# Fused adaLN, attention-like mixer and mixture-of-experts kernel: the last four tiles kept on chip for the shared expert, their reload taken out, and three orders of work moved

## The chip, the cores and the metric

The kernel runs on one core of one Trainium2 chip. The metric is device time in microseconds of one execution. Engines are named as in the profile: PE (TensorE), DVE (VectorE), ACT (ScalarE), POOL (GpSimd), SP (SyncE, which here only issues transfers).

## The reference, cut to what matters

There are 2048 tokens of 512 values, 8 experts of which each token takes 2, and a shared expert of twice an expert's hidden width (2 x 352). All is float32.

```python
mod = (_silu(L0_c) @ L0_wmod).reshape(L0_c.shape[0], 6, 1, -1)
sa, ca, ga, sb, cb, gb = ...
h = _layernorm(x, axis=-1) * (1 + ca) + sa
x = x + ga * _L0_attn_ref(h, B, C, D)     # tanh(h B^T) C^T + D * h
h = _layernorm(x, axis=-1) * (1 + cb) + sb
x = x + gb * _L0_ffn_ref(h, ...)
# in _L0_ffn_ref:
scores = jax.nn.sigmoid(logits)
_, idx = jax.lax.top_k(scores + router_bias, K)
y = jnp.einsum('eth,ehd->etd', jax.nn.silu(h1) * h3, W2)
out = jnp.einsum('etd,te->td', y, gate_full) + shared
```

## The kernel before

Tokens are cut into 16 tiles of 128, and tiles into 8 pairs. Each float32 product is made of three matmuls on a high and a low part (high x high, high x low, low x high), so every operand is held twice: `xah`, `xal` or `thi`, `tlo` (also called `xbh`, `xbl`) for tokens, `whi`, `wlo` for weights.

The program has an opening (modulation vectors, weights of the first stages) and then four stages.

**Stage A** runs over the pairs, as a software pipeline of 11 rounds (`body(it, lo, hi)` on each engine, `it` from 0 to 10). In round `it` the engines normalise pair `it`, turn the normalised pair `it - 1` and compute its states (`turn_t`, `states`), make the mixer's output for pair `it - 2` (`attention`), and for pair `it - 3` turn the second normalisation `h2` and run the first half of the shared expert (`up("A", ...)`, `down("A", ...)`, with the router's columns beside the up product). Rounds 3, 4, 8, 9 and 10 are written out, rounds 5 to 7 are a loop. `h2` of each pair goes to DRAM (`hs_rows`), comes back, and is scattered by GpSimd to rows sorted by expert (`xs_rows`, four indirect transfers a pair). The turned `h2` in its two parts goes to DRAM too (`store_x` to `xt_high`, `xt_low`).

**Stage B** runs the second half of the shared expert on four tiles, here tiles 0 to 3, which `load_x` fetches from `xt_high` and `xt_low`: two at the start of round 10, the third when the first tile's up product is done, and the fourth after the second's.

**Stage S** runs the routed experts on blocks of 128 rows of `xs_rows`, two steps in a loop. **Stage C** runs the second half of the shared expert on the other 12 tiles, fetches for each tile its two routed results (`gather`), combines and stores. The four tiles of stage B and the last two of stage C are combined apart: `gather_first` fetches their routed rows, `weigh` on ACT multiplies the first by its weight, and three operations on DVE (`combine`) end them.

A step of stages B, S and C is on PE: the up product of tile n (24 matmuls), the down product of tile n - 1 (9 matmuls), the turn of the gated hidden values of tile n (3 transposes). In stage S the turn of the next block (4 transposes) stands ahead of it. ACT makes silu and the high part of the hidden values, DVE the product and the low part. The order on each engine is written by hand, and semaphores alone order the engines.

In the profile, the up product is lines 1007 to 1009, the down product 1038 to 1040, the turn of the hidden values 1045, all other transposes 984, the mixer's products 953 to 955, and the modulation 962. The wait that guards a fetched tile is the first line of `up`:

```python
if loaded is not None:
    pe.wait_ge(q["C", "xin"][j], loaded * 32)
```

On ACT the turned pair may be overwritten in `xah` once `store_x` has read it:

```python
if lo > 3:
    act.wait_ge(q["A", "up"], p * 2)
    act.wait_ge(s_xts, p * 32)
```

## Time and profile before

| What | Value |
|---|---|
| median of 3 runs | 570.36 us (569.66 to 571.24) |
| profiled execution: its time | 571.33 us |
| its span, first to last instruction | 569.7 us |
| PE busy | 543.4 us (95%) |
| DVE, POOL, ACT busy | 286.6, 263.5, 176.3 us |
| mean granted TensorE clock | 0.990 of full |
| transfers | 119.80 MB, mean 210 GB/s |

PE is busy for 95% of the span, so the time is that of PE's work and of the gaps in it. A gap is seen as a small digit of PE in the 40 slices of the page, as less than the length of a stretch in its busy time, and in the list of PE's instructions as the number in brackets behind the instruction that came late, with what released it. "issue" in a bracket means that the profile names no releaser. A matmul's duration in such a list is longer than the distance to the next start, since matmuls overlap, so paces are read from starts.

### The profile page before, as it was taken

The numbers are of one execution on the slowest core, as the hardware profiler recorded it, in microseconds if no ns is written. First come the engines' busy times: TensorE is split into PE (matmuls) and PEld (weight loads), VectorE is DVE, ScalarE is ACT, GpSimd is POOL, SyncE is SP. The second block draws the span as 40 slices with busy tenths as digits, with TensorE's granted clock in tenths as the row PEclk, the third lists the DMA queues.
The fourth block names the chain that finished last, engine by engine and source line by source line (L and its number), as shares of the span: only waits on it lengthen the run. The fifth ranks groups of instructions, "written<-read, shape, count | busy, mean of one in ns | idle before, by whom it ended". The sixth has DMA issues, their size and how long they took to land.

```text
span 569.7 us, 11068 instructions
## 1 busy us (share of the span) xinstructions
PE 543.4 (95%) x3129; PEld 487.3 (86%) x3130; DVE 286.6 (50%) x612; ACT 176.3 (31%) x337; POOL 263.5 (46%) x221
## 2 busy tenths in 40 slices
PE   8996899999999995999999999999999999988997
PEld 3665788998999894999999999999999999987896
DVE  3788586686687565442222222222222222158897
ACT  1444345445534330122223222322223223112211
POOL 2599877668666457343016260044443300254630
PEclk9999899999999998999999999999999999999999
DMA  8999266543452889566254946255758313475982
GB/s 309 395 337 382 84 212 249 186 160 116 166 191 106 286 316 375 190 220 227 96 161 157 326 138 231 74 175 192 288 167 310 129 55 110 152 257 188 314 306 79
DMA packets 47915, 119.80 MB, mean 210 GB/s; under 512 B 4752, under 2 KB 5008, under 8 KB 47888
## 3 DMA queue, kind: packets, MB, share of 16 engines
q1 hardware_dynamic: 35088, 67.02, 33.4%
q0 software_dynamic: 12800, 52.43, 26.0%
q8 instruction: 15, 0.25, 0.2%
q14 instruction: 12, 0.10, 0.1%
HBM read 80.38 MB, written 39.06 MB: 210 GB/s over the span
## 4 chain that ended last, share of the span: by engine, by line
PE 79%; POOL 7%; issue 5%; DMA 4%; DVE 3%; ACT 1%; SPq 0%; POOLq 0%; DVEq 0%; ACTq 0%
PE bank L1007 14%; PE bank L1009 14%; PE bank L1008 14%; PE bank L1038 8%; PE bank L1040 7%; PE bank L1039 7%; PE bank L984 4%; PE bank L1045 4%; PE bank L955 2%; PE bank L953 2%; PE bank L954 2%; DMA x_all<-wmod 2%; POOL tmpa L595 1%; DMA xt_low<-xal 1%; POOL x_all L598 1%
## 5 line engine op out<-in xcount | busy, mean ns | idle before, releaser
L1007 PE MATMUL bank<-whi,thi 128*128 (+1 forms) x416 | 139.9, 336 | 8.3 <-issue 8.3
L1008 PE MATMUL bank<-wlo,thi 128*128 (+1 forms) x416 | 135.9, 327 | 0.0
L1009 PE MATMUL bank<-whi,tlo 128*128 (+1 forms) x416 | 135.5, 326 | 0.0
L582 POOL TENSOR_TENSOR wlo<-raw,whi 128x1408 f32 (+3 forms) x24 | 79.6, 3329 | 83.7 <-DMA whi<-w_all 74.0
L1007 PEld LDWEIGHTS bank<-whi,thi 128*128 128x128 f32 x416 | 79.5, 191 | 9.0 <-issue 9.0
L1742 DVE TENSOR_TENSOR gbuf<-s,bank 128x352 f32<-128x352 f32 x52 | 27.0, 520 | 112.5 <-ACT s L927 111.5
L1038 PE MATMUL bank<-whi,gth 128*128 (+1 forms) x201 | 79.9, 397 | 2.3 <-DVE gtl L1305 1.3
L1040 PE MATMUL bank<-whi,gtl 128*128 (+1 forms) x201 | 79.0, 393 | 0.0
L1008 PEld LDWEIGHTS bank<-wlo,thi 128*128 128x128 f32 x416 | 79.0, 190 | 0.0
L1009 PEld LDWEIGHTS bank<-whi,tlo 128*128 128x128 f32 x416 | 78.9, 190 | 0.0
L1039 PE MATMUL bank<-wlo,gth 128*128 (+1 forms) x201 | 78.8, 392 | 0.0
L927 ACT ACTIVATE s<-bank 128x352 f32<-128x352 f32 x52 | 24.1, 464 | 159.9 <-PE bank L1009 156.5
L1760 DVE TENSOR_TENSOR gtl<-bank,gth 128x384 fp32r<-128x384 f32 x51 | 28.4, 556 | 79.0 <-ACT gth L936 73.8
L936 ACT ACTIVATE gth<-bank 128x384 fp32r<-128x384 f32 x51 | 25.1, 491 | 96.0 <-PE bank L1045 93.8
L1040 PEld LDWEIGHTS bank<-whi,gtl 128*128 128x128 f32 x201 | 37.8, 188 | 8.9
L1038 PEld LDWEIGHTS bank<-whi,gth 128*128 128x128 f32 x201 | 37.9, 189 | 8.6 <-issue 2.9
L1007 PE MATMUL bank<-whi,xah 128*128 128x360 f32 (+1 forms) x128 | 42.3, 330 | 1.4 <-DVE xal L1472 1.3
L1039 PEld LDWEIGHTS bank<-wlo,gth 128*128 128x128 f32 x201 | 37.8, 188 | 5.8
L553 POOL DMA_DIRECT2D whi<-w_all x21 | 11.4, 552 | 66.5 <-PE bank L1009 66.3
L1009 PE MATMUL bank<-whi,xal 128*128 128x360 f32 (+1 forms) x128 | 41.6, 325 | 0.0
L1008 PE MATMUL bank<-wlo,xah 128*128 128x360 f32 (+1 forms) x128 | 41.6, 325 | 0.0
L1045 PEld LDWEIGHTS bank<-cst,gbuf 128*128 128x128 f32 x204 | 25.9, 140 | 16.1 <-issue 4.3
(222 smaller groups left out, 951.8 us busy)
## 6 DMA issues: line engine op xcount, KB each, us to landing
raw<-w_all POOLq DMA_DIRECT2D x8, 2176.0 KB
whi<-w_all POOLq DMA_DIRECT2D x16, 704.0 KB, 11.5
h<-xs_rows SPq DMA_DIRECT2D x36, 256.0 KB, 2.7
ys_rows<-tmpa SPq DMA_DIRECT2D x36, 256.0 KB, 2.0
x_all<-wmod SPq DMA_DIRECT2D x6, 1024.0 KB, 9.7
whi<-w_all POOLq DMA_DIRECT2D x8, 768.0 KB, 4.6
hs_rows<-h SPq DMA_DIRECT2D x8, 512.0 KB, 5.1
xt_high<-xah SPq DMA_DIRECT2D x8, 512.0 KB
```

Of the source, the lines that this page charges most:

```text
L582: pool.tensor_tensor(wlo[:, bass.ds(off + (SH + a), b - a)], raw[:, a:b], whi[:, bass.ds(off + (SH + a), b - a)].bitcast(F32), ALU.subtrac ...
L927: act.activation(s1[:, :], bank[2][:, 0:F], ACT.Silu).then_inc(q["S", "silu"], 1)
L936: act.activation(gth_b if last else gth[:, :], bank[4][:, 0:FP], ACT.Copy).then_inc(q["S", "ghi"], 1)
L1007: pe.matmul(dst, xh[:, j, a], wh, start=(m == 0), stop=False)
L1008: pe.matmul(dst, xh[:, j, a], wl, start=False, stop=False)
L1009: mm = pe.matmul(dst, xl[:, j, a], wh, start=False, stop=(m == KD - 1))
L1038: pe.matmul(dst, gth[:, a], wh, start=(m == 0), stop=False)
L1039: pe.matmul(dst, gth[:, a], wl, start=False, stop=False)
L1040: mm = pe.matmul(dst, gtl[:, a], wh, start=False, stop=(m == KF - 1))
L1045: mm = pe.transpose(dst[:, m * P:(m + 1) * P], gbuf[:, m * P:(m + 1) * P], ident)
L1742: dve.tensor_tensor(gbuf[:, 0:F], s1[:, :], bank[3][:, 0:F], ALU.mult).then_inc(q["S", "g"], 1)
L1760: dve.tensor_tensor(gtl_b if last else gtl[:, :], bank[4][:, 0:FP], (gth_b if last else gth[:, :]).bitcast(F32), ALU.subtract).then_inc(q[ ...
```

## The change

Stage B now works on tiles 12 to 15, the last two pairs of stage A. Their turned parts are still on chip: pair 6 stays in `xah`, `xal`, and pair 7 is put into `xbh`, `xbl`, so `store_x` stops after pair 5 and stage B fetches nothing. Stage C works on tiles 0 to 11, with four places for fetched tiles in place of two (`xt_place`), so a tile is asked for four steps ahead; the first two are asked for early in stage S. In stage C, `gather_first` starts one slot earlier, `weigh` comes behind the copy to `gth` and not ahead of it, its steps are 2, 4, 5, 7, 8, 10 in place of 3, 4, 6, 7, 9, 10, and the 18 parts of `combine` lie on other steps, the last of them after `finish_last(0, 0, 1)`. PE's stage C is written out whole; before, its steps 4 to 9 were a loop. In round 3 the turn of pair 2 stands ahead of `h2` of pair 0 and the mixer of pair 1, in banks 2 and 3 in place of 6 and 7. The split of the router's columns moves from the opening's third round to its end on ACT and DVE.

```diff
-FIRST_LAST = [*range(NB), *range(NT - NL, NT)]
-WEIGH_AT = [3, 4, 6, 7, 9, 10]
+NC = NT - NB
+FIRST_LAST = [*range(NC, NT), *range(NC - NL, NC)]
+WEIGH_AT = [2, 4, 5, 7, 8, 10]
+COMBINE_AT = [(), (), (), (0, 1), (2,), (3, 4), (5, 6), (7, 8), (9, 10), (11, 12), (13, 14), (15, 16)]
...
+        xt_place = [(xah, xal, 0), (xah, xal, 1), (xbh, xbl, 0), (xbh, xbl, 1)]
...
                 if lo == NP + 2:
-                    sp.wait_ge(s_stp, NP)
-                    sp.wait_ge(s_xts, 32 * (NP - 1))
-                    for t in range(2):
-                        load_x(t, t)
                     sp.wait_ge(s_nat, NP * 16)
...
-                if live(3, lo, hi):
+                if live(3, lo, hi) and lo <= NP:
                     store_x(it - 3)
...
-                if k < NT - NB:
-                    sp.wait_ge(q["S", "up"], iters * 2 + (NB + k - 1))
-                    load_x(NB + k, k % 2)
+                if k < NC:
+                    sp.wait_ge(q["S", "up"], iters * 2 + (NB + k - 3))
+                    load_x(k)
...
-            for t in range(2, NB):
-                sp.wait_ge(q["S", "up"], t - 1)
-                load_x(t, t % 2)
-            sp.wait_ge(s_xts, 32 * NP)
...
+            sp.wait_ge(s_xts, 32 * (NP - 2))
+            sp.wait_ge(q["S", "up"], 2)
+            for t in range(2):
+                load_x(t)
...
-                    for t in range(2):
-                        pool.wait_ge(q["C", "xin"][t], 32)
...
+                if lo > 3 and not (lo == NP + 1 and p == NP - 1):
                     act.wait_ge(s_xts, p * 32)
-                for j in range(2):
-                    act.activation(xah[:, j, :], h2_bank(lo, j)[:, :], ACT.Copy).then_inc(q["A", "xhi"], 1)
+                dst = xbh if lo == NP + 1 and p == NP - 1 else xah
+                for j in range(2):
+                    act.activation(dst[:, j, :], h2_bank(lo, j)[:, :], ACT.Copy).then_inc(q["A", "xhi"], 1)
...
-                if k in WEIGH_AT:
-                    weigh(WEIGH_AT.index(k))
                 act.wait_ge(q["S", "gt"], i * 2 + (j + 1))
...
                 act.activation(gth_b if last else gth[:, :], bank[4][:, 0:FP], ACT.Copy).then_inc(q["S", "ghi"], 1)
+                if k in WEIGH_AT:
+                    weigh(WEIGH_AT.index(k))
...
                 if loaded is not None:
-                    pe.wait_ge(q["C", "xin"][j], loaded * 32)
+                    xh, xl = xt_place[loaded % 4][0:2]
+                    if loaded >= 4:
+                        pe.wait_ge(s_xl[loaded % 4], 32 * (loaded // 4))
+                    else:
+                        pe.wait_ge(q["A", "xlo"], NT)
...
-                if live(1, lo, hi) and lo != 3:
+                if live(1, lo, hi):
                     turn_t(it - 1, lo)
...
-                if lo == 3:
-                    turn_t(it - 1, lo)
...
-            iters = steps(pe, step, lambda: pairs_of_b(pe))
+            iters = steps(pe, step, lambda: pairs_of_b(pe), True)
...
                 if last:
                     dve.wait_ge(q["S", "dn"], i * 2 + j)
                     finish_last(0, 0, 1)
+                    combine(NB + NL - 1, 2)
```

Three places are shown as they stand on their engines. The first is SP between rounds 9 and 10 of stage A and the first fetch of stage S (`h2<-xs_rows`); `mods` and `tmpa` take `hs_rows` on its way to the scatter. Before:

```order
L451 DMA hs_rows<-h2 128x2x512
L415 DMA mods<-hs_rows 128x2x512
L425 DMA xt_high<-xah 128x2x512
L425 DMA xt_low<-xal 128x2x512
L451 DMA hs_rows<-h2 128x2x512
L420 DMA thi<-xt_high 128x512
L420 DMA tlo<-xt_low 128x512
L420 DMA thi<-xt_high 128x512
L420 DMA tlo<-xt_low 128x512
L415 DMA tmpa<-hs_rows 128x2x512
L415 DMA mods<-hs_rows 128x2x512
L425 DMA xt_high<-xah 128x2x512
```

Behind these came the other store, the fetches of the third and fourth tile, and then `h2<-xs_rows`. Of the change:

```order
L449 DMA hs_rows<-h2 128x2x512
L416 DMA mods<-hs_rows 128x2x512
L449 DMA hs_rows<-h2 128x2x512
L416 DMA tmpa<-hs_rows 128x2x512
L416 DMA mods<-hs_rows 128x2x512
```

All stores of pairs 6 and 7 and all fetches of four tiles are gone, and the next transfer is `h2<-xs_rows`.

The second is PE at round 3, behind the last product of the modulation (`x_all` holds its weights, `h2` is pair 0, `tbuf` pair 2, `chi` the mixer of pair 1). Before:

```order
L962 MATMUL bank7<-x_all,big3 128x512
L984 MATMUL bank4<-cst,h2 128x128 x4
L984 MATMUL bank5<-cst,h2 128x128 x4
L953 MATMUL bank0<-chi,shi 128x512
L954 MATMUL bank0<-clo,shi 128x512
L955 MATMUL bank0<-chi,slo 128x512
...
L984 MATMUL bank6<-cst,tbuf 128x128 x4
L984 MATMUL bank7<-cst,tbuf 128x128 x4
L1007 MATMUL bank2<-whi,xah 128x360
```

Of the change:

```order
L957 MATMUL bank7<-x_all,big3 128x512
L979 MATMUL bank2<-cst,tbuf 128x128 x4
L979 MATMUL bank3<-cst,tbuf 128x128 x4
L979 MATMUL bank4<-cst,h2 128x128 x4
L979 MATMUL bank5<-cst,h2 128x128 x4
L948 MATMUL bank0<-chi,shi 128x512
```

The eight transposes of pair 2 have moved from behind the mixer's twelve matmuls to ahead of everything in the round.

The third is ACT in stage C, steps 2 to 4 (`s1` is silu, `gth` the high part of the hidden values, `raw<-raw` is `weigh`). Before:

```order
L927 ACTIVATE s1<-bank2 128x352
L936 ACTIVATE gth<-bank4 128x384
L922 REGISTER_ALU
L927 ACTIVATE s1<-bank2 128x352
L911 ACTIVATE raw<-raw,zrow,wts 128x512
L936 ACTIVATE gth<-bank4 128x384
L922 ISA
L927 ACTIVATE s1<-bank2 128x352
L911 ACTIVATE raw<-raw,zrow,wts 128x512
L936 ACTIVATE gth<-bank4 128x384
```

Of the change:

```order
L922 ACTIVATE s1<-bank2 128x352
L929 ACTIVATE gth<-bank4 128x384
L906 ACTIVATE raw<-raw,zrow,wts 128x512
L917 REGISTER_ALU
L922 ACTIVATE s1<-bank2 128x352
L929 ACTIVATE gth<-bank4 128x384
L917 ISA
L922 ACTIVATE s1<-bank2 128x352
L929 ACTIVATE gth<-bank4 128x384
L906 ACTIVATE raw<-raw,zrow,wts 128x512
```

`weigh` has moved from between silu and the copy to `gth` of its step to behind that copy, and the first of them one step earlier.

## Rows read from the trace of the kernel before

**Rows 1.** Busy time by 20 us stretch; last: PEclk, DMA share, GB/s.

```profile
220.00:240.00 20.00, 14.40 (x71) 13.73 (x72) 7.13 (x21) 2.02 (x4) 11.75 (x6) 0.83 0.65 233
240.00:260.00 20.00, 20.00 (x121) 18.73 (x120) 9.32 (x21) 5.04 (x10) 9.91 (x5) 1.00 0.64 224
```

**Rows 2.** Chain that ended last, around round 9: start us, us, what.

```profile
180.96 3.48 DMA xs_rows<-mods,idx
...
185.44 5.92 DMA xt_low<-xal
...
191.47 0.60 ACT xah L777
```

**Rows 3.** PE in order of time, rounds 9 and 10.

```profile
188.09 1.04 PE L984 MATMUL bank<-cst,h 128*128 128x128 f32 x8
...
192.93 0.40 PE L1007 MATMUL bank<-whi,xah 128*128 128x360 f32 x1 [1.28 <-DVE xal L1472]
```

**Rows 4.** PE in order of time, stage B, third tile.

```profile
225.60 0.63 PE L1007 MATMUL bank<-whi,thi 128*128 128x352 f32 x1 [6.45 <-issue]
...
230.81 0.32 PE L1007 MATMUL bank<-whi,thi 128*128 128x352 f32 x1
...
231.78 0.40 PE L1038 MATMUL bank<-whi,gth 128*128 128x512 f32 x1
```

**Rows 5.** Chain that ended last: the turn of the first block of stage S.

```profile
234.35 0.44 PE bank L984 x4
```

**Rows 6.** SP in order of time: transfers issued.

```profile
203.07 0.38 SPq L415 DMA_DIRECT2D mods<-hs_rows  x1
...
209.92 0.35 SPq L420 DMA_DIRECT2D thi<-xt_high  x1
...
227.99 20.75 SPq L412 DMA_DIRECT2D h<-xs_rows  x5
```

**Rows 7.** Line 412 (blocks of stage S), its first three transfers.

```profile
DMA to landing us min/median/max: 2.6/3.0/5.4
```

**Rows 8.** Line 490, SP's wait for the last scatter: durations ns, first and last start us.

```profile
L490 SPq EVENT_SEMAPHORE  x1: 17/17/17, 226.8 to 226.8; - x1
```

**Rows 9.** POOL in order of time: the scatter of pair 7.

```profile
214.25 0.96 POOL L658 DMA_INDIRECT xs_rows<-mods,idx  x1 [3.17 <-DMA mods<-hs_rows]
...
218.07 0.96 POOL L658 DMA_INDIRECT xs_rows<-mods,idx  x1 [0.30 <-issue]
```

**Rows 10.** Busy time by stretch, stage C; columns of rows 1.

```profile
476.50:508.20 31.70, 31.70 (x184) 29.40 (x182) 11.13 (x22) 6.25 (x13) 9.27 (x9) 1.00 0.50 163
508.20:551.20 43.00, 38.85 (x219) 34.94 (x217) 32.55 (x62) 9.36 (x17) 22.43 (x22) 1.00 0.80 274
```

**Rows 11.** PE in order of time, stage C, instructions that came late.

```profile
510.06 0.42 PE L1007 MATMUL bank<-whi,thi 128*128 x1 [1.71 <-issue]
515.17 0.49 PE L1038 MATMUL bank<-whi,gth 128*128 x1 [1.00 <-DVE gtl L1760]
518.53 0.55 PE L1045 MATMUL bank<-cst,gbuf 128*128 128x128 f32 x3 [1.02 <-DVE gbuf L1742]
```

**Rows 12.** Chain that ended last, stage C, step 3.

```profile
505.78 5.12 DMA raw<-ys_rows,idxb
...
512.24 0.82 ACT raw L911
```

**Rows 13.** PE in order of time, round 3.

```profile
44.27 1.06 PE L984 MATMUL bank<-cst,h 128*128 128x128 f32 x8 [1.47 <-issue]
...
56.30 0.73 PE L1045 MATMUL bank<-cst,gbuf 128*128 128x128 f32 x3 [3.29 <-DVE gbuf L1301]
```

**Rows 14.** ACT in order of time: pair 2 normalised.

```profile
44.86 1.52 ACT L823 ACTIVATE tbuf<-x_all,nm,rs 128x512 f32<-128x512 f32 x2 [3.95 <-POOL nm L613]
```

**Rows 15.** DVE in order of time: second normalisation of pair 1; last part of `combine`.

```profile
64.42 1.42 DVE L1569 SCALAR_TENSOR_TENSOR h<-h,rs,mods 128x512 f32<-128x512 f32 x2 [3.22 <-POOL rs L625]
...
562.77 0.69 DVE L1687 TENSOR_TENSOR mods<-mods,x_all 128x512 f32<-128x512 f32 x1
```

More of the change, by code:

```diff
@@ L191, in build @@
         rowb += [h2, mods[:, 0:2, :]]
-        gth_b, gtl_b = xah[:, 0, 0:FP], xah[:, 1, 0:FP]
+        gth_b, gtl_b = (t[:, :, :].rearrange("p a b -> p (a b)")[:, 0:FP] for t in (shi, slo))
+        xt_place = [(xah, xal, 0), (xah, xal, 1), (xbh, xbl, 0), (xbh, xbl, 1)]
         btr = xtf[:, :, :].rearrange("p b d -> p (b d)").rearrange("p (k n) -> p k n", k=KD)
@@ L247, in build @@
         s_xts = sem("s_xts")
+        s_xl = [sem(f"s_xl{b}") for b in range(4)]
         s_lg = sem("s_lg")
@@ L266, in build @@
                 q[sec, n] = sem(f"{n}_{sec}")
-            q[sec, "xin"] = [sem(f"xin{j}_{sec}") for j in range(2)]
+            if sec == "S":
+                q[sec, "xin"] = [sem(f"xin{j}_{sec}") for j in range(2)]
             q[sec, "ydma"] = [sem(f"ydma{j}_{sec}") for j in range(2)]
@@ L755, in _ @@
                 gather(CB, j)
+            for k in range(2):
+                gather_first(0, k)
             for c in range(CB + 1, NP - 1):
@@ L894, in _ @@
             magnitude(5)
+            act.wait_ge(l_gate, 32)
+            act.activation(whi_a[:, :, 0:E], gw[:, :, :], ACT.Copy).then_inc(s_gwh, 1)
             iterations(act, body, 3)
@@ L1104, in body @@
             def body(it, lo, hi):
-                if live(1, lo, hi) and lo != 3:
+                if live(1, lo, hi):
                     turn_t(it - 1, lo)
@@ L1129, in body @@
                         pe.wait_ge(s_gwl, 1)
-                    if live(1, lo, hi) and lo > 3:
+                    if live(1, lo, hi):
                         pe.wait_ge(s_tlo, (it - 1) * 2 + 2)
@@ L1229, in step @@
                 up("S", i, j, off, [NW + 1, NW + 2] if sec == "B" else need_up,
-                   i + 1 if sec == "B" else c + 1 if sec == "C" else None, last)
+                   i * 2 + j if sec == "B" else 4 + (c - CB) * 2 + j if sec == "C" else None, last)
                 if first:
@@ L1469, in lows_a @@
             def lows_a(p, lo):
+                high_, low_ = xah, xal
+                if lo == NP + 1 and p == NP - 1:
+                    dve.wait_ge(s_stp, NP)
+                    high_, low_ = xbh, xbl
                 for j in range(2):
                     dve.wait_ge(q["A", "xhi"], p * 2 + (j + 1))
-                    dve.tensor_tensor(xal[:, j, :], h2_bank(lo, j)[:, :], xah[:, j, :].bitcast(F32),
+                    dve.tensor_tensor(low_[:, j, :], h2_bank(lo, j)[:, :], high_[:, j, :].bitcast(F32),
                                       ALU.subtract).then_inc(q["A", "xlo"], 1)
@@ L1711, in finish @@
                     dve.wait_ge(q["C", "ydma"][j], (c - CB) * 16)
-                w = [wts[:, c * 2 + j:c * 2 + j + 1, k] for k in range(2)]
+                w = [wts[:, n - 1:n, k] for k in range(2)]
                 dve.scalar_tensor_tensor(y, tbuf[:, j, :], w[0], bank[5 + j][:, :],
@@ L1748, in step @@
                 if m >= 0:
-                    for n in range(2 * m, 2 * m + 2):
+                    for n in COMBINE_AT[m + 3]:
                         combine(n // 3, n % 3)
```

60 lines of the change are left out of this document (24 added, 36 removed).

## The prediction

> **What bounds the kernel now.** I read the busy time by 20 us stretches first. From 240 to 260 us, and in every stretch on to 500, PE is busy throughout at the full clock; from 220 to 240 it is busy for only 14.40 us at a mean clock of 0.83 [rows 1]. So stage S can't be shortened by this change, and its steps only move in time. What counts are the gaps around it. Next I read PE's list for brackets, and then the chain of waits for what stands behind each.
>
> Gap 1, round 9. PE comes 1.28 us late to the first up product of pair 7, released by the low part on DVE [rows 3]. The chain says why: after the transfer of `xt_low` landed (185.44 + 5.92 = 191.36) ACT could overwrite `xah`, and DVE followed [rows 2]. The transposes that ACT copies from had ended at 189.13 [rows 3].
>
> Gap 2, stage B. PE waits 6.45 us for its third tile and then runs at half the pace [rows 4]. The profile names no releaser, but the code has one candidate: that tile's fetch, issued at 209.92 [rows 6], the only wait of `up` that isn't an engine's. The 18 matmuls from 225.60 to 230.81 took 5.21 us, 0.289 each; the six from there to 231.78 took 0.97, 0.162 each, which is the full clock.
>
> Gap 3, stage C. In 476.5 to 508.2 PE runs without a gap, 184 instructions in 31.70 us, 0.172 each. In 508.2 to 551.2 there are 219, which at that pace take 37.7 us, but the stretch has 43.0 [rows 10]: 5.3 us are lost. Three waits make 3.73 of it [rows 11]. The first is at the first matmul of an up product. The second and third come from one thing: `weigh` waited for its gathered rows, 5.12 us in transfer, until 512.24 [rows 12], with the copy to `gth` behind it on ACT; so the low part on DVE was late, then the down product, then `finish` on DVE and the next hidden values behind it.
>
> Gap 4, the opening. PE waits 1.47 us for `h2` of pair 0 and 3.29 for hidden values in round 3 [rows 13].
>
> **The change part by part.** *Round 9.* The wait on the store goes, since pair 7 goes to `xbh`. ACT can start at 189.15; from its start to PE's there were 192.93 - 191.47 = 1.46 us [rows 2, 3], so PE could go on at 190.6, before it is done with its round at 192.93 - 1.28 = 191.65 [rows 3]. Gain 1.28. Pair 7's place is the one that the states' operands left, one round ago; no new wait.
>
> *Stage B.* No fetch, so 6.45 goes, and with it the slow clock: the up product took 231.78 - 225.60 = 6.18 us and should take 24 x 0.162 = 3.89, gain 2.29 [rows 4]. Add some 0.1 for the slow start of a first matmul. Together 8.8, and with round 9 10.1: PE would stand before the turn of stage S's first block at 234.35 - 10.1 = 224.2 [rows 5].
>
> *What is late next.* That turn needs a block of `xs_rows`, which SP may fetch once all scatters have landed. Its fetch was issued at 227.99 [rows 6] and took between 2.6 and 5.4 us [rows 7], so PE's gap hid it. The chain in front: SP fetches `hs_rows` of pair 7 at 203.07 [rows 6]; POOL waits for it, 3.17 us, until 214.25, and issues its last scatter at 218.07 [rows 9]. Everything that starts that chain is behind the gap of 1.28, so 218.07 becomes 216.8. A scatter's last transfer took 3.48 when little else ran [rows 2]: 220.3. From the end of that wait to the fetch SP took 227.99 - 226.8 = 1.2 [rows 6, 8], in which it reads the row number: 221.5. Landing at 2.6 to 3.0: 224.1 to 224.5. So PE waits about 0.3 us; I take 0.5. The two ends: nothing, if the fetch of pair 7 lands sooner; and 5.5, if the scatter lands as late as before (227.99 - 1.28 + 3.0 = 229.7 against 224.2). I lean to the low end, since 2 MB of transfers (two stores of 512 KB and four fetches of 256 KB) no longer run beside the scatter, which took 226.8 - 218.07 = 8.7 us to land with them and 3.48 in the quiet stretch.
>
> The 11 us from 203.07 to 214.25 for one 512 KB transfer are the long part [rows 6, 9], with POOL's weight transfers under way and nothing ahead in SP's own queue. I do not shorten it, since what is taken away stood behind it. The Trainium skill, "DMA: Bandwidth & Descriptors", section "Queues, rings and completion order", says that each DMA engine takes turns between the queues it has work for, a packet at a time. By that rule removing later transfers of SP's queue gives this one nothing, and the wait of 0.5 stays; by bytes alone it would land earlier, and the wait would be nothing.
>
> *Stage C.* Tiles are asked for four steps ahead: the one behind the wait of 1.71 now goes out before step 1 and not at the end of step 2, into transfer engines that are half idle (share 0.50 against 0.80) [rows 10]. That wait goes. `weigh` stands behind the copy to `gth`, so its wait no longer holds the copy back; its rows are asked for some 5 us earlier and it has until the next silu. The waits of 1.00 and 1.02 go [rows 11]. Of the 5.3 us I take 4.4: the three waits, and 0.7 of the 1.6 beside them, the part that is restart behind them. The rest, small delays of 0.2 to 0.4 in later steps with the transfers busy, I leave standing. Bounds 3.7 and 5.3; if the last two waits only move by a step, 1.7.
>
> *The end.* The last part of `combine` (0.69 [rows 15]) now stands on DVE between the last two tiles' ends, on the chain that sets the end. I take a loss of 0.4, bounds 0 and 0.7.
>
> *PE's stage C written out.* The same instructions, no jumps. Nothing in the trace prices fetching them: the ends of stage A and stage B are written out too, and show no wait of PE but those named. Zero, with 1.71 [rows 11] as the upper end, should that wait have been one for code.
>
> *Round 3.* The turn of pair 2 needs `tbuf`, ready at 44.86 + 1.52 = 46.38 [rows 14]. PE was free at 44.27 - 1.47 = 42.80 [rows 13], so its wait becomes 3.6 in place of 1.47 and all it does in the round comes 46.38 - 44.27 = 2.1 us later (the eight transposes of pair 2 only change places). Behind stands a gap of 3.29 us [rows 13], whose hidden values wait on ACT for POOL's product on the raw weights. So 2.1 disappears there. DVE's second normalisation of pair 1, which decides the next round, waits 3.22 for POOL [rows 15], which this change doesn't touch; its input comes 2 us later and still in time. Zero, bounds -0.2 and +1.5. A rule speaks against the move: after the wait of 6.45 PE ran at half the pace for some 5 us [rows 4], which cost 2.3, and a wait of 3.6 may do the same here: 2.1 + 2.3 = 4.4, of which 3.29 are hidden and up to 1.1 are not. "TensorE: Matmul & The Clock Gate", section "Part 1: The HAM clock gate" in the Trainium skill, states that PE falls to half its clock when idle. By that rule the term is +1.1 at most, by the gap alone 0. I keep 0, since the products behind it then run without the gap that slowed them.
>
> Sum: 10.1 - 0.5 + 4.4 - 0.4 = 13.6 us. From the profiled execution's 571.33 that gives 557.7; it ran 0.97 above the median of the runs, so in their terms 570.36 - 13.6 = 556.8.
>
> **The rivals.** *The scatter lands as late as before.* For it: the 3.17 us that POOL waited and a stretch in which transfers are saturated. Against: less to move. A new wait of 5.5 us before the first block, and 2.3 of slow clock: 556.8 - 0.5 + 7.8 = 564.1; half of it is 560. Chance 0.17.
>
> *Stage C's waits move and don't go.* DVE is busy for 32.55 of 43.0 us there [rows 10] and each step puts two parts of `combine` between two things that PE needs. Then only 1.7 is gained in place of 4.4: 559.5. Chance 0.12.
>
> *Slower.* PE's written-out steps of stage C wait for code while the transfer engines are busy. Six steps were in the loop; if each waited more than 13.6 / 6 = 2.3 us, the change loses. At 1.71 a step, 10.3, the time is 567.1; at 2.5, 571.8. Against it: stage B, written out, under saturated transfers, has none. Chance 0.03 for the losing size, 0.01 for one within 0.3% of it.
>
> *The change does nothing to the gap in stage B*, because it wasn't the fetch. Then 8.8 stays: 565.6. Chance 0.03. Mine has the other 0.64.
>
> **How the numbers follow.** Mine alone spans 554.5 (stage C's full 5.3, no new wait, no loss at the end, 0.2 in round 3: 556.8 - 0.9 - 0.5 - 0.4 - 0.2 = 554.8) to 559 (1.1 in round 3, another 1 us before the first block). The range goes to 562, which takes in the second rival and the milder half of the first; left out are its full size, the fourth and the loss. 0.3% of 570.36, 1.7 us, is about what can be told from no change; every case but the slower one is faster by more than that, 0.96 in all.
>
> **What would show it.** In the trace of the changed kernel: no bracket at the first up product of pair 7; none at the third tile of stage B, clock 1.00 there; a bracket of under 1 us at the turn of the first block (line 979); stage S without gaps; in stage C no bracket at an up product, and `weigh` ending before the next silu; in round 3 a bracket of 3.6 at the turn of pair 2 and one under 1.2 at the hidden values. I would be wrong by most if the first block's turn had a bracket of several us.

## The result, and the profile after

The changed kernel takes 563.21 us (median of 4 runs, 561.89 to 564.70) against 570.04 in the runs beside it. The ratio is 0.9873, 95% interval 0.9844 to 0.9901: a gain of 6.8 us, half of the 13.6 forecast, and 1.2 us outside the range. The profiled execution took 561.89 us, the lowest of the four, with a span of 560.2 us and a mean clock of 0.994; against the profiled execution of before it gains 9.4 us.

Where it came from is read by places that both traces have. The busy time by stretch of the changed kernel, with the columns of [rows 1]; the last two stretches have the lengths of those in [rows 10] and begin 10.4 us earlier, as stage C does:

```profile
220.00:240.00 20.00, 19.29 (x114) 17.47 (x113) 13.28 (x29) 4.68 (x9) 9.99 (x6) 1.00 0.58 200
466.06:497.76 31.70, 29.79 (x172) 27.37 (x170) 7.24 (x14) 5.35 (x12) 10.26 (x10) 1.00 0.53 167
497.76:540.76 43.00, 40.48 (x224) 36.60 (x225) 35.43 (x69) 10.08 (x19) 21.38 (x21) 1.00 0.77 259
```

From 220 to 240 us PE now works 19.29 of 20 us at the full clock, where it had 14.40 at 0.83. In stage C it does not: 1.91 us are idle in the stretch that had no gap before, and 2.52 in the one behind it.

PE in order of time around the first two blocks of stage S (line 979 is the turn of a block, 1046 that of hidden values):

```profile
222.61 0.60 PE L979 MATMUL bank<-cst,h 128*128 128x128 f32 x4
...
229.57 0.55 PE L1046 MATMUL bank<-cst,gbuf 128*128 128x128 f32 x3 [0.39 <-DVE gbuf L1740]
230.44 0.63 PE L979 MATMUL bank<-cst,h 128*128 128x128 f32 x4 [0.32 <-issue]
```

The first turn has no bracket: the fetch that I feared for was in time. The second comes 7.83 us after the first, where the third comes 6.78 after the second, so 1.05 us are lost one step later than I had looked. SP and POOL on the way there, in order of time:

```profile
199.87 0.38 SPq L416 DMA_DIRECT2D mods<-hs_rows  x1
...
218.11 13.47 SPq L413 DMA_DIRECT2D h<-xs_rows  x4
```

```profile
210.25 0.96 POOL L654 DMA_INDIRECT xs_rows<-mods,idx  x1 [1.84 <-DMA mods<-hs_rows]
...
214.13 0.96 POOL L654 DMA_INDIRECT xs_rows<-mods,idx  x1 [0.30 <-issue]
```

The transfer for the scatter was asked for 3.2 us earlier and POOL went on 10.4 us after it (11.2 before [rows 6, 9]). The fetch for the block went out at 218.11, 3.4 us ahead of the 221.5 that I had worked out.

The 1.05 us are DVE's. Between the low part and the next hidden values (`gbuf`) it makes the routing's weights and positions. One product of that work, and what POOL does beside it:

```profile
225.74 2.48 DVE L1643 TENSOR_TENSOR st<-oh,sc 128x256 f32<-128x256 f32 x1
```

```profile
221.25 6.69 POOL L580 TENSOR_TENSOR wlo<-raw,whi 128x1408 fp32r<-128x1408 f32 x2
```

The same product in the trace of before:

```profile
237.32 0.42 DVE L1645 TENSOR_TENSOR st<-oh,sc 128x256 f32<-128x256 f32 x1
```

It stands at the same place in DVE's order there, behind PE's gap, and by then POOL's split of weights had ended (at 232.99).

And stage C, PE's instructions around its gaps, with two ends of up products (line 1010) for comparison:

```profile
482.63 0.33 PE L1010 MATMUL bank<-whi,xal 128*128 x1
...
488.94 0.32 PE L1010 MATMUL bank<-whi,tlo 128*128 x1
...
493.01 0.55 PE L1046 MATMUL bank<-cst,gbuf 128*128 128x128 f32 x3 [1.67 <-issue]
...
499.00 0.50 PE L1039 MATMUL bank<-whi,gth 128*128 x1 [1.49 <-issue]
...
502.31 0.55 PE L1046 MATMUL bank<-cst,gbuf 128*128 128x128 f32 x3 [0.95 <-DVE gbuf L1740]
```

With one of 0.25 at 515.41 the brackets make 4.36 us. ACT's instructions that take those products:

```profile
482.99 0.47 ACT L922 ACTIVATE s<-bank 128x352 f32<-128x352 f32 x1 [2.87 <-PE bank L1010]
...
491.94 0.47 ACT L922 ACTIVATE s<-bank 128x352 f32<-128x352 f32 x1 [6.03 <-remote]
497.72 0.49 ACT L929 ACTIVATE gth<-bank 128x384 fp32r<-128x384 f32 x1 [5.31 <-remote]
```

This is the line on which the result turns. At step 1 the last matmul of the up product ends at 482.63 + 0.33 = 482.96 and silu begins at 482.99. At step 2 it ends at 489.26 and silu begins at 491.94, 2.68 us late; "remote" in the bracket means that the profile found no instruction that ended when the wait did. The copy to `gth` begins 4.2 us after the transposes that it reads (493.01 + 0.55). ACT did nothing in between, DVE was waiting for this silu, and the signals of ACT and DVE came on time in the middle of it:

```profile
492.44 0.52 DVE L1740 TENSOR_TENSOR gbuf<-s,bank 128x352 f32<-128x352 f32 x1 [2.01 <-issue]
```

DVE begins 0.03 us after silu has ended (491.94 + 0.47 = 492.41), and PE's turn begins at 493.01, 0.05 us after DVE has ended (492.44 + 0.52 = 492.96). Neither the fetched tiles nor `weigh` stand ahead of the two late instructions on ACT. The records that the trace keeps of semaphore updates say the same: that of the up product's last matmul is at 491.92, that of the down product behind it, whose last matmul is shown to end at 491.34, at 497.63, and that of the turn at 497.68. Elsewhere in the program a matmul's update follows its shown end by 0.01 us in the median, and so do those of ACT and DVE that are recorded. Not every update is: where one is missing, the next is a whole step or more behind, and it says nothing. So PE had done its work, by the trace, and the others were not told. "Perfetto Trace Analysis" in the Trainium skill, section "Summary: the profiler window per engine type", says that the end shown for TensorE is an estimate and that the time for a semaphore to spread is outside what the profiler reports. The trace agrees that the lateness is in no instruction's duration. It is not the estimate that is off: the updates at 497.63 and 497.68 lie 0.05 us apart and the work behind them 2.2 us, so they were held and then let go together.

What POOL did meanwhile:

```profile
483.35 1.03 POOL L738 DMA_INDIRECT tbuf<-ys_rows,idx  x1 [41.60 <-issue]
...
495.41 0.95 POOL L744 DMA_INDIRECT raw<-ys_rows,idxb  x1 [0.30 <-issue]
```

Ten indirect transfers in a row, each 0.30 us after the one before, from 483.35 to 496.36. Before, there were four here, then a pause of 3.0 us.

By place, profile against profile: the opening +1.30 us (`h2` of round 4 turned at 69.98, before at 71.28), round 9 and stage B +10.3 (first block's turn at 222.61 in PE's list, before at 234.19 there; the chain of [rows 5] starts it 0.16 later), the second block -1.05, the rest of stage S -0.1, stage C -0.6 (silu of step 0 gained 10.41, that of step 11 9.84), the end -0.4. The sum is 9.4.

All of this rests on one profile of the kernel before, and its stages are not the same in every execution. The two runs on the opening, further down, have its code from round 4 on. PE's gap at the third tile of stage B is 4.53 and 4.52 us in them and not 6.45:

```profile
222.70 0.63 PE L1001 MATMUL bank<-whi,thi 128*128 128x352 f32 x1 [4.53 <-issue]
```

The way from the turn of `h2` in round 4 to that of the first block is 162.91 us in the profile of before, 159.93 and 159.76 in these two, and 152.63 in the changed kernel (152.61 to 152.88 in its three profiles). Stage C, from silu of step 0 to silu of step 11, takes 72.48, 74.94 and 76.25 us, and 73.05 in the changed kernel (73.01 to 73.07). So the gain of round 9 and stage B is 10.3 by one profile and 7.1 to 7.3 by the two others, and that of stage C is -0.6 by one and +1.9 and +3.2 by the others. How the 6.8 of the medians is shared between the two stages is known no better than that.

### The profile page after: what moved, and what is told of

The parts are those of the page before. It is cut to its first block, busy times and chain, and to the rows that moved or that the text cites. A ratio compares the mean times of both kernels' runs of the same rounds, so it can differ in the third digit from the quotient of the medians.

```text
span 560.2 us, 11029 instructions
## 1 busy us (share of the span) xinstructions
PE 542.0 (97%) x3129; PEld 485.9 (87%) x3130; DVE 291.0 (52%) x612; ACT 176.8 (32%) x337; POOL 262.8 (47%) x221
## 3 DMA queue, kind: packets, MB, share of 16 engines
q0 software_dynamic: 12800, 52.43, 27.1%
## 4 chain that ended last, share of the span: by engine, by line
PE 88%; DVE 4%; another core or an unknown queue 2%; issue 2%; ACT 1%; DMA 1%; SPq 0%; DVEq 0%; ACTq 0%
PE bank L1010 15%; PE bank L1008 15%; PE bank L1009 15%; PE bank L1039 8%; PE bank L1041 8%; PE bank L1040 8%; PE bank L979 5%; PE bank L1046 4%; PE bank L948 3%; PE bank L949 3%; PE bank L950 3%; PE bank L957 3%; DMA x_all<-wmod 1%; DVE gtl L1301 1%
## 5 line engine op out<-in xcount | busy, mean ns | idle before, releaser
L1008 PE MATMUL bank<-whi,thi 128*128 (+2 forms) x368 | 122.8, 334 | 0.0
L1009 PE MATMUL bank<-wlo,thi 128*128 (+2 forms) x368 | 119.6, 325 | 0.0
L1010 PE MATMUL bank<-whi,tlo 128*128 (+2 forms) x368 | 119.1, 324 | 0.0
L1008 PEld LDWEIGHTS bank<-whi,thi 128*128 128x128 f32 x368 | 69.7, 189 | 0.0
L1009 PEld LDWEIGHTS bank<-wlo,thi 128*128 128x128 f32 x368 | 69.1, 188 | 0.1
L1010 PEld LDWEIGHTS bank<-whi,tlo 128*128 128x128 f32 x368 | 69.1, 188 | 0.0
L1008 PE MATMUL bank<-whi,xah 128*128 128x352 f32 (+2 forms) x176 | 58.3, 331 | 0.1
L1009 PE MATMUL bank<-wlo,xah 128*128 128x352 f32 (+2 forms) x176 | 57.2, 325 | 0.0
L1010 PE MATMUL bank<-whi,xal 128*128 128x352 f32 (+2 forms) x176 | 57.1, 325 | 0.0
L738 POOL DMA_INDIRECT tbuf<-ys_rows,idx x10 | 11.2, 1115 | 61.0 <-issue 44.3
```

The lines of the kernel that those rows point to most:

```text
L1008: pe.matmul(dst, xh[:, j, a], wh, start=(m == 0), stop=False)
L1009: pe.matmul(dst, xh[:, j, a], wl, start=False, stop=False)
L1010: mm = pe.matmul(dst, xl[:, j, a], wh, start=False, stop=(m == KD - 1))
```

## The experiments

**The changed kernel again, and the order of stage C as before.** Two theories of the gap at step 2 were open: the row of ten indirect transfers, and ACT itself being late, for its code or anything else of its own. First the same program once more.

> The changed kernel once more, unedited, for a second profile. If the four gaps of stage C (1.67, 1.49, 0.95 and 0.25 us, together 4.36) come from how the gathers of this kernel stand, the second profile has gaps of 3 to 6 us in sum at the same steps (k = 2 and k = 5). If they were an accident of one execution, they are elsewhere or gone. The time should be 563, 0.987 of the kernel before.

563.59 us against 569.36, ratio 0.9882 (0.9836 to 0.9928). Its gaps in stage C:

```profile
495.82 0.55 PE L1046 MATMUL bank<-cst,gbuf 128*128 128x128 f32 x3 [3.06 <-issue]
...
503.68 0.55 PE L1046 MATMUL bank<-cst,gbuf 128*128 128x128 f32 x3 [0.96 <-DVE gbuf L1740]
...
516.81 0.55 PE L1046 MATMUL bank<-cst,gbuf 128*128 128x128 f32 x3 [0.31 <-DVE gbuf L1740]
```

4.33 us in sum, 4.36 in the first profile, at the same steps (2, 3 and 5; the 1.49 of the down product is not there, and the first is longer by as much). It is no accident.

```diff
-WEIGH_AT = [2, 4, 5, 7, 8, 10]
-COMBINE_AT = [(), (), (), (0, 1), (2,), (3, 4), (5, 6), (7, 8), (9, 10), (11, 12), (13, 14), (15, 16)]
+WEIGH_AT = [3, 4, 6, 7, 9, 10]
+COMBINE_AT = [(), (), ()] + [(2 * m, 2 * m + 1) for m in range(9)]
...
-            for k in range(2):
-                gather_first(0, k)
             for c in range(CB + 1, NP - 1):
                 for j in range(2):
                     gather(c, j)
-                    n = (c - CB - 1) * 2 + j + 1
+                    n = (c - CB - 1) * 2 + j
...
                 act.activation(s1[:, :], bank[2][:, 0:F], ACT.Silu).then_inc(q["S", "silu"], 1)
...
+                if k in WEIGH_AT:
+                    weigh(WEIGH_AT.index(k))
...
                 act.activation(gth_b if last else gth[:, :], bank[4][:, 0:FP], ACT.Copy).then_inc(q["S", "ghi"], 1)
-                if k in WEIGH_AT:
-                    weigh(WEIGH_AT.index(k))
...
                     finish_last(0, 0, 1)
-                    combine(NB + NL - 1, 2)
```

> The changed kernel with the order of stage C as before (gather_first a slot later, weigh ahead of the copy to gth at steps 3, 4, 6, 7, 9, 10, combine's parts two a step from step 3, none behind finish_last); the four places for tiles stay. Theory 1, ten gathers in a row hold up what PE signals: the run of ten becomes one of four and one of eight, the 2.7 us at silu of step 2 and the 4 us at gth of step 2 go, the old waits of 1.0 and 1.0 behind weigh come back, the end gains 0.4; the gap sum of stage C is 2 to 3.5 and the time 561 to 563. Theory 2, the new order is better than the old whatever the gathers: 563 + 1 to 2 = 564 to 565. Theory 3, ACT is late on its own code: the gap stays at the same step.

563.34 us, ratio 0.9880 (0.9837 to 0.9923): the whole new order of stage C is worth nothing that can be measured. The gap at step 2 is gone. ACT's code changed with the order, so this speaks against a delay of ACT's own and does not settle it; the extra gathers below, which leave ACT's code as it is, do. Beside one of 0.35 us there is another, at the down product, behind `weigh` on ACT. PE's instruction and then ACT's two:

```profile
505.34 0.49 PE L1037 MATMUL bank<-whi,gth 128*128 x1 [3.15 <-issue]
```

```profile
502.34 0.81 ACT L904 ACTIVATE raw<-raw,zrow,wts 128x512 f32<-128x512 f32 x1 [5.53 <-DMA raw<-ys_rows,idxb]
503.06 0.47 ACT L929 ACTIVATE gth<-bank 128x384 fp32r<-128x384 f32 x1
```

So the new place of `weigh` does take a wait away, and the new place of `gather_first` puts one of the same size there. The wait of 1.71 at an up product [rows 11] is in neither, with the four places for tiles in both.

**Plain transfers in place of indirect ones.** Only `gather_first` is edited. It fetches 128 rows that follow one another, which are not the rows that the routing asks for, so this kernel computes something else for six tiles.

```diff
-                pool.indirect_dma_start(rowb[t][:, k, :], None, ys[:, :],
-                                        bass.IndirectOffsetOnAxis(ap=idxb[:, 2 * t + k:2 * t + k + 1], axis=0)
-                                        ).then_inc(s_brow[t], 16)
+                n = 2 * t + k
+                pool.dma_start(rowb[t][:, k, :], ys[n * P:(n + 1) * P, :]).then_inc(s_brow[t], 16)
```

> gather_first fetches 128 consecutive rows with a plain transfer in place of an indirect one; the same bytes at the same places of the order, other rows than the reference's for six tiles, so this part of the result is different data. If indirect transfers of POOL, one behind another, hold up PE's signals, then the run at step 2 is of four and not of ten, the gaps of 1.67 and 1.49 go and the time falls by 2 to 3 us against the changed kernel (560 to 561). If it is the bytes in flight (DMA share 0.7 to 0.9), they stay within 1 us of 3.2, and the time at 562 to 564. If it is ACT's code, they stay too.

557.52 us (557.22 to 557.99), ratio 0.9779 (0.9736 to 0.9822), 6.1 us under the changed kernel beside it, where I had expected 2 to 3. PE has no gap in stage C at all; the 4.4 us of brackets are gone, and what made the other 1.7 is not shown. The same two stretches as above:

```profile
466.06:497.76 31.70, 31.70 (x183) 29.39 (x183) 11.44 (x24) 7.07 (x14) 8.36 (x10) 1.00 0.54 177
497.76:540.76 43.00, 43.00 (x249) 40.13 (x248) 35.87 (x67) 9.04 (x17) 20.44 (x22) 1.00 0.82 281
```

Transfers are as dense (share 0.54 and 0.82, against 0.53 and 0.77), and POOL's queue carries the same 12,800 packets and 52.43 MB in both. What differs is how they are issued:

```profile
488.45 0.95 POOL L738 DMA_INDIRECT xtf<-ys_rows,idx  x1 [0.31 <-issue]
489.40 1.18 POOL L745 DMA_DIRECT2D raw<-ys_rows  x2
492.42 1.12 POOL L738 DMA_INDIRECT tbuf<-ys_rows,idx  x1 [1.83 <-DVE idx L1665]
```

Two plain ones take POOL 1.18 us, two indirect ones 2.5. So the same bytes and packets through the same queue hold nothing back when fewer of them are issued by indirect instructions. With that POOL's rows also became shorter: six, then four at a time (two indirect, two plain) with pauses of 1.8 us and more. A row of ten plain transfers was not run, so this run does not tell the indirect instruction from the time that POOL spends issuing.

**Extra gathers where nothing waits.** In stage S, behind the last weights, POOL issues ten gathers that nobody needs (`s_try` is a semaphore of their own).

```diff
             pool.wait_ge(w_ready, split)
+            pool.wait_ge(s_bidx, 2)
+            for n in range(10):
+                pool.indirect_dma_start((rowb[n // 2][:, n % 2, :] if n < 8 else (tbuf, xtf)[n % 2][:, 0, :]), None,
+                                        w_all.rearrange("a f -> (a f)").rearrange("(n d) -> n d", d=D),
+                                        bass.IndirectOffsetOnAxis(ap=idxb[:, n:n + 1], axis=0)).then_inc(s_try, 16)
+            pool.wait_ge(s_try, 160)
```

> The changed kernel with ten more indirect gathers of 256 KB in stage S, at about 442 us, where no step of PE waits; they read a weight tensor into tiles that nothing uses then. If a row of ten indirect gathers holds up PE's signals by several us, PE has brackets of 1 to 5 us in sum between 445 and 470, at turns of hidden values and down products, with ACT's silu or gth late behind a matmul that had ended. If lateness needs something else of stage C, PE stays without a gap there. Span 560 to 565.

571.18 us in one run, 7.6 over the changed kernel beside it; the span of 569.5 is 4.5 above what I had expected at most. PE, ACT and the last of the ten on POOL:

```profile
451.60 0.32 PE L1017 MATMUL bank<-whi,tlo 128*128 x1
...
459.26 0.90 PE L1053 MATMUL bank<-cst,gbuf 128*128 128x128 f32 x3 [5.26 <-DVE gbuf L1747]
```

```profile
458.18 0.46 ACT L929 ACTIVATE s<-bank 128x352 f32<-128x352 f32 x1 [9.08 <-remote]
```

```profile
443.81 1.03 POOL L730 DMA_INDIRECT raw<-w_all,idxb  x1 [0.86 <-POOL wlo L581]
...
455.20 0.94 POOL L730 DMA_INDIRECT xtf<-w_all,idxb  x1 [0.30 <-issue]
```

The up product ends at 451.92 and silu takes it at 458.18, 6.3 us late and 2.0 after POOL's last issue ends. PE then runs slow for a while, its mean clock 0.78 from 460 to 470. From the turn of the first block to silu of stage C's step 0 it takes 261.89 us, against 254.12 in the changed kernel. This was the cause by itself, in a part of stage S in which no step of PE waits (its only brackets are the 0.39 and 0.32 at the second block).

The same with four (`range(4)`), and with ten rows of half the width (256 values, `d=256`):

> As the run with ten extra gathers in stage S, but with four. If the row must be longer than four before PE's signals are held up, PE has no bracket between 440 and 470. If each transfer costs its share, there is one of 4/10 of the 5.26 us that ten gave, 2.1 us.

> The run with ten extra gathers in stage S, each of 128 rows of 1 KB in place of 2 KB: as many indirect transfers and as long a row on POOL (some 12 us), half the bytes. If the number of indirect transfers issued in a row holds up PE's signals, PE has again a bracket of 4 to 6 us between 450 and 462. If it is the bytes that pile up behind them, the bracket is under 1 us.

With four (563.96 us in one run) PE has no bracket there, and the same way takes 254.11 us; from 440 to 460 PE is busy throughout:

```profile
440.00:460.00 20.00, 20.00 (x120) 18.73 (x120) 5.20 (x9) 5.80 (x12) 6.84 (x5) 1.00 0.36 118
```

With ten of half the bytes (575.14 us in one run) the bracket is there again:

```profile
459.32 0.48 PE L1053 MATMUL bank<-cst,gbuf 128*128 128x128 f32 x1 [4.89 <-DVE gbuf L1747]
```

4.89 against 5.26 us: bytes hardly count, the number in a row does. The two runs with ten extra gathers also kept a row of ten in stage C, and what that one cost was less steady: a wait of 4.25 us in the run with 2 KB rows, and 7.22 in the run with 1 KB rows, where silu began 8.2 us late:

```profile
508.03 0.90 PE L1053 MATMUL bank<-cst,gbuf 128*128 128x128 f32 x3 [7.22 <-DVE gbuf L1747]
```

**Breaking the row.** Three kernels try to keep the gathers and lose the row. The first has `weigh` behind `gth` at steps 3, 4, 6, 7, 9, 10, `combine` a step later, and a wait ahead of every `gather_first`:

```diff
             for c in range(CB + 1, NP - 1):
                 for j in range(2):
+                    n = (c - CB - 1) * 2 + j
+                    if n < NB + NL:
+                        pool.wait_ge(s_gath[1 - j], 32 * ((n + 1) // 2 + 1))
+                        for k in range(2):
+                            gather_first(n, k)
                     gather(c, j)
```

> The changed kernel with every transfer kept indirect, but never more than four of POOL's in a row: each gather_first first waits until the gather before it has landed; weigh at steps 3, 4, 6, 7, 9, 10, still behind gth, combine's parts a step later. If the length of a row of indirect transfers is what holds up PE's signals, the gaps in stage C (3.1 in one step and 4.3 in sum in the second profile of the changed kernel) fall under 1 us in sum, and the time goes to 558 to 560. If it is each indirect transfer by itself, the gaps stay at 3 to 4 us in sum and the time at 562 to 564. If the waits make the rows late instead, ACT's weigh holds back silu or gth by 1 us or more at some steps, and the time is over 563.

580.29 us, ratio 1.0151 (1.0126 to 1.0176): slower than the kernel before. No recorded signal of PE in stage C is late by more than 0.06 us in its trace, with rows of four, one of six, and pauses of 3 us and more between them, so the cause is taken away, but the wait that does it costs more than it saves. POOL, and what DVE and PE then wait for:

```profile
503.56 0.95 POOL L744 DMA_INDIRECT raw<-ys_rows,idxb  x1 [5.72 <-DMA xtf<-ys_rows,idx]
```

```profile
514.30 0.75 DVE L1710 SCALAR_TENSOR_TENSOR tmpa<-tbuf,wts,bank 128x512 f32<-128x512 f32 x1 [5.52 <-PE bank L1040]
```

```profile
517.90 0.90 PE L1045 MATMUL bank<-cst,gbuf 128*128 128x128 f32 x3 [4.40 <-DVE gbuf L1739]
```

Four transfers take 5 us to issue and 5.7 to land, some 11 us for what a step of 6.3 us asks for; DVE's `finish` waits for its rows (the releaser that the bracket names had long been done), and `gbuf` behind it.

The second only puts `gather_first` a slot later than the changed kernel, so that the rows are of four and eight (the loop as in the second experiment, `weigh` behind `gth`):

> The changed kernel with gather_first a slot later, as before, so that POOL's first row is of four and the next of eight, and not ten; weigh stays behind the copy to gth, at steps 3, 4, 6, 7, 9, 10, and combine's parts lie one step later (2 a step from step 4, 3 at the last). If a row of ten is what costs, and weigh ahead of gth cost the 3.15 us in the run with the old order, then both go here: PE's gaps in stage C under 1.5 us in sum, signals late by under 1 us, time 559 to 561, 2 to 4 us under the changed kernel. If weigh's place has no part in it, a gap of 3 us stays at the down product of step 3 and the time is 563.

560.64 us (558.90 to 566.55), ratio 0.9833 (0.9782 to 0.9883). Its gaps in stage C:

```profile
505.97 0.55 PE L1044 MATMUL bank<-cst,gbuf 128*128 128x128 f32 x3 [0.48 <-DVE gbuf L1738]
...
519.29 0.55 PE L1044 MATMUL bank<-cst,gbuf 128*128 128x128 f32 x3 [0.52 <-DVE gbuf L1738]
```

With one of 0.38 they are 1.38 us in place of 4.3. A fourth, of 0.59 at the last down product, waits for DVE, which has three parts of `combine` in the last step here. Stage C takes 69.3 us in place of 73.1. Its times spread more than those of the others, two of the six at 566, so the intervals overlap, and the 2.7 us under the changed kernel are likely, not shown. It has the lowest median of those kernels here that compute the whole reference.

The third adds one wait to it, `pool.wait_ge(s_brow[n - 1], 32)` ahead of each `gather_first(n, k)` but the first:

> The run with gather_first a slot later, and each gather_first also waits until the one before it has landed, so that POOL pauses 1 to 2 us in a row of eight and at most six transfers are under way, without the idle 5.8 us of the run with four in a row. If a pause is enough, PE's signals are late by under 0.5 us at most, the gaps of stage C sum to under 0.8 us and the time is 559 to 560.5. If the rows come late instead, ACT's weigh or DVE's finish hold up gbuf and the time is 562 or more.

562.28 us (558.44 to 565.11), ratio 0.9852 (0.9821 to 0.9883), no better. One row of eight with pauses of 0.46 us at most remained in it, and there the old picture is back:

```profile
522.38 0.55 PE L1046 MATMUL bank<-cst,gbuf 128*128 128x128 f32 x3 [3.64 <-DVE gbuf L1740]
```

while ACT waits 5.2 us for rows in an earlier step. So pauses of that length don't help here, and longer ones made the rows late in the run before.

**The opening.** The first profile had gained 1.30 us there, where I had forecast nothing. Each of its two parts was put alone into the kernel before: the turn of pair 2 (shown for PE; ACT, DVE and the banks follow it), and the split of the router's columns.

```diff
-                if live(1, lo, hi) and lo != 3:
+                if live(1, lo, hi):
                     turn_t(it - 1, lo)
...
-                if lo == 3:
-                    turn_t(it - 1, lo)
```

> The kernel before with one part of the change alone: in round 3 the turn of pair 2 stands first, in banks 2 and 3; the router's split stays where it was. If the 1.3 us that the changed kernel gained by round 4 come from DVE's second normalisation of pair 1 no longer running beside POOL's two products (3.46 and 4.45 us for two each before, 1.40 and 2.52 after), because the turn's copies stand ahead of it on DVE, then those durations appear here too and h2's transposes of round 4 start at 70.0 in place of 71.3. If the router's split (2.35 us on DVE) is what moves it, they stay at 3.46 and 4.45. The time: 569.4 - 1.3 = 568.1, or no change.

> The kernel before with the other part of the opening alone: the split of the router's columns at the end of the opening on ACT and DVE. If the turn's place is the cause, nothing moves at round 4 (71.3); if the split is, h2's transposes of round 4 start at 70.0.

The turn alone: 572.17 against 571.69, ratio 1.0005 (0.9983 to 1.0026), `h2` of round 4 at 71.08. The split alone, 572.60 in one run: at 71.82. Neither brings the 1.30 in its one profile. Then the third profile of the changed kernel:

> The changed kernel once more beside it: a third profile and time. The theory of the row of ten wants a gap of 1.5 to 4.5 us at the turn of step 2 again, and 562 to 564 us. In the opening, h2's transposes of round 4 start at 71.3, or at 70.0 when DVE's split of the mixer's weights happens to run at 3.8 us and its normalisation after POOL's products; both have been seen of this same program.

563.31 us, ratio 0.9882 (0.9866 to 0.9899), a bracket of 3.06 at step 2 again, and `h2` of round 4 at 70.12; in the second it was at 71.30. In DVE's list of the two, the second and then the third:

```profile
60.30 3.55 DVE L1547 SCALAR_TENSOR_TENSOR h<-x_all,mv,mods 128x512 f32<-128x512 f32 x2
```

```profile
62.64 1.40 DVE L1547 SCALAR_TENSOR_TENSOR h<-x_all,mv,mods 128x512 f32<-128x512 f32 x2
```

One program, two courses. DVE and POOL work side by side on tiles of the same size there; either DVE's normalisation runs beside POOL's sum (3.55 for two on DVE, 3.80 on POOL in place of 2.4) or DVE's split before it takes 3.7 to 4.0 us in place of 2.5 and the normalisation comes alone. Of the eleven profiles with the changed opening four took the second course. So 1.3 us of the first profile's 9.4 were luck. Its 9.4 stand 2.6 us above the 6.8 of the medians. By the times, 1.3 of them are that the profiled execution of before took more than the median beside the result, and 1.3 that the changed kernel's took less; the second course of the opening is as large as the latter and likely its cause.

## Why the prediction was half right

*Round 9 and stage B*, forecast 10.1: 10.3 measured against the profile from which it was worked out. No bracket in round 9, none at the third tile, the clock at 1.00. Right in mechanism. The size is less sure than it looks: the gap of 6.45 was the longest of three, and against the other two profiles of that code the gain is 7.1 to 7.3.

*What is late next*, forecast -0.5 at the first block's turn, with 5.5 as the far end: nothing there. All my bounds were about transfers. The fetch went out 3.4 us before I had it, of which 1.3 are the opening's luck; in the second profile it went out at 221.19, 0.3 before, and its block was still in time for the turn at 224.18. Taking SP's later transfers away did not bring the scatter's rows sooner: POOL went on 10.4 and 10.5 us after the request in the two runs on the opening, which still have those transfers, and 10.4 and 10.7 in two profiles of the changed kernel. A loss of 1.05 came a step later, from DVE's product of 2.48 us beside POOL's split of weights. In PE's gap of 6.45 that split had run out, and the product behind the gap took 0.42. It is 2.46 to 2.51 us long in all eleven profiles with stage B's change, and 0.42 in all three without it. The size was off by 0.6, and the place was one that I had not priced: the gap had kept DVE and POOL apart.

*Stage C*, forecast +4.4: -0.6 against the profile of before (+1.9 and +3.2 against the other two), and this is the step that failed. What I said of the waits was right: with four places for tiles no up product waits, and with `weigh` behind `gth` the waits of 1.00 and 1.02 are gone. But I priced "its rows are asked for some 5 us earlier" at nothing. Asking earlier joined four gathers and six into one row of ten, and such a row holds back what PE signals: ten in stage S cost a wait of 5.3 us by themselves, four cost nothing, and with plain transfers of the same bytes through the same queue nothing is held back in stage C. With that taken out, stage C gains: from silu of step 0 to that of step 11 it takes 67.2 us in the run with plain transfers, 73.05 in the changed kernel and 72.48 before. That is 5.3, the upper end that I had given, and more against the other two profiles of the code of before. That run's 557.5 us stands 0.7 from the 556.8 forecast, but it is another kernel, and with the sizes above as unsure as they are the agreement is in part chance. One reading was also off: I had the rows of `weigh` in transfer until 512.24, while the chain ends their transfer at 510.89 and leaves 1.34 us without a name; nothing in the sum hangs on it.

*The end*, forecast -0.4: -0.4 (8.18 us from the last silu to DVE's end, 7.76 before). *Round 3*, forecast 0: +1.30 in the first profile, 0.9 to 1.3 in three more, and -0.4 to +0.1 in the other seven; right for most executions and 1.2 off in the rest. The waits came as forecast, 3.82 us at the turn of pair 2 (3.6) and 1.20 at the hidden values (1.2 at most). PE did run slow after the first: its mean clock is 0.77 from 50 to 55 us, where before it was 1.00, and 1.00 from 55 to 60, where before it was 0.66. So the rival that PE slows after such a wait was right in its mechanism, and its cost was hidden by the wait behind it. *PE's written-out code*, forecast 0: in the run with plain transfers PE has no gap in stage C, so nothing.

*The rivals.* The second, stage C's waits move and don't go, named the right stage; its cause, DVE's load, was the wrong one, and its price of 2.7 was half of the 5 that the first profile shows. The first was given more chance and cost nothing. What I could have seen: in the trace of before, ACT already began late behind matmuls that had ended, by 1.2 to 1.4 us at 526.72 and 530.51, while POOL issued a row of eight and just behind it. I read only PE's brackets and took the 1.6 us beside the three waits for restarts.

What stays open is what in the chip holds the signals back, why PE's and not those of ACT and DVE, and whether ten plain transfers in a row would do it too. The runs show that the lateness grows with the row, not the point at which it begins. With ten in a row the latest signal of PE came 5.9 to 8.2 us late, in every one of the eight such rows. With eight it was 0.4 to 1.9 in most and 2.2 to 4.6 in five rows, two in each of the runs on the opening, whose order of stage C is that of before. With four it was nothing in stage S and nothing in the run that waits before every group, but 0.4 to 1.3 behind rows of four in stage C of other kernels, most of which had pauses of 0.8 to 2.1 us before them. So four in a row are not free everywhere, and the number is not all that counts.

## What to carry to other kernels

For each stage take the distance from an engine's last instruction to the start of the one that waits for it, in a step that runs well, and compare it in the steps around a gap; when it grows by microseconds and nothing else is named, the signal is late and not the work. Moving transfers earlier is not free even when their queue has room: count how many indirect ones then stand in a row on POOL, and try groups of four with pauses between them. The pauses have a price as well: the run that waited before every group lost more than it gained. And when a gap is closed, list what every engine did in it, and which work of two engines will now fall together, before looking at transfers alone. A second profile of the same program tells whether a gain of 1 us is one. That holds for the kernel before too: a gap read as 6.45 us in one profile was 4.5 in two others of the same code.

## What the runs showed of the hardware

- A row of ten indirect transfers on POOL, most of 0.95 us and 0.30 apart, made PE's signals arrive up to 6.3 us late in three profiles of the changed kernel, 6.2 in a stage where nothing else was changed, and 8.2 at most in all. Those of ACT and DVE came on time where a step in the middle of the row shows them (0.03 and 0.05 us). The last of PE's were let go 1.3 to 2.4 us after POOL had issued the row's last transfer.
- Ten of 1 KB rows did the same as ten of 2 KB rows in stage S (brackets of 4.89 and 5.26 us), four of 2 KB rows did nothing there. In stage C some rows of four went with signals 0.4 to 1.3 us late, without a bracket of over 0.4 us on PE.
- Two plain transfers of 256 KB take POOL 1.18 us to issue, two indirect ones 2.5. "DMA: Bandwidth & Descriptors" in the Trainium skill, section "SWDGE vs HWDGE vs iDMA", says that GpSimd computes the descriptors of all of its transfers in software, plain ones too; the profile agrees in that both are counted in the one software queue. By that alone they would be alike for PE; in the run with six pairs of plain ones PE's signals were on time, though its rows were also shorter.
- A product on DVE of 128x256 took 0.42 us with POOL idle and 2.46 to 2.51 beside POOL's subtraction on 128x1408, and ended 0.3 us after it.
- Two engines working on large tiles side by side can fall into two courses in one program, 1.2 us apart at round 4 here. Four of eleven profiles took the second, and two of three of one and the same program.
